# Causal mask, row scale and row extreme of attention scores in one VectorE pass per token tile

## The reference, cut to what matters

```
q = rms_norm((x @ Wq).reshape(B, S, 16, 128), gq)
k = rms_norm((x @ Wk).reshape(B, S, 4, 128), gk)      # then each repeated 4 times
attn = einsum('bqhd,bkhd->bhqk', q, k) * 128 ** -0.5
attn = where(causal, attn, -inf);  attn = softmax(attn, axis=-1)
out = einsum('bhqk,bkhd->bqhd', attn, v).reshape(B, S, 2048) @ Wo
```

## Time and profile before

| | |
|---|---|
| median of 3 runs | 1098.98 us (1098.12 to 1102.88) |
| the profiled execution | 1098.61 us |
| its span, first to last instruction | 1096.7 us |
| PE (matmuls) busy | 1002.0 us, 91% |
| DVE busy | 729.3 us, 66% |
| ACT busy | 691.1 us, 63% |
| mean granted clock of TensorE | 0.961 of full |

### The profile page before, as it was taken

The page is one execution under the profiler, slowest core; times in us unless marked ns, Lnnn a source line. Parts: engine busy times, 40 slices in busy tenths (PEclk is TensorE's granted clock), DMA queues, the critical chain, the costliest instruction groups (busy, mean ns, idle before and its releaser), DMA issues.

```text
span 1096.7 us, 20605 instructions
## 1 busy us (share of the span) xinstructions
PE 1002.0 (91%) x6148; PEld 837.5 (76%) x6148; DVE 729.3 (66%) x2417; ACT 691.1 (63%) x1944; POOL 427.8 (39%) x450
## 2 busy tenths in 40 slices
PE   7999999999999999999999999985788688999990
PEld 4668888877887788887887788864567587999990
DVE  3564656777748766774884686765677666888880
ACT  2567767777767676866776686663544346676760
POOL 3222411425412541541263253231064643666663
PEclk9999999999999999999999999997789799999995
DMA  9919992986894200110021031227066678899964
GB/s 312 284 61 332 378 376 73 354 299 252 301 377 149 109 20 1 65 64 1 1 90 40 1 131 55 84 93 251 11 166 158 172 167 224 220 228 228 232 144 77
DMA packets 93725, 180.47 MB, mean 165 GB/s; under 512 B 9949, under 2 KB 29085, under 8 KB 92717
## 3 DMA queue, kind: packets, MB, share of 16 engines
q1 hardware_dynamic: 73467, 148.55, 40.6%
q0 software_dynamic: 18800, 30.24, 12.0%
q10 hardware_dynamic: 1346, 0.36, 0.2%
HBM read 77.58 MB, written 107.99 MB: 169 GB/s over the span
## 4 chain that ended last, share of the span: by engine, by line
PE 78%; DVE 8%; DMA 4%; issue 3%; ACT 3%; another core or an unknown queue 1%; POOL 1%; SPq 0%; DVEq 0%; ACTq 0%; POOLq 0%
PE bank L1071 11%; PE bank L1007 10%; PE bank L1035 9%; PE bank L1080 6%; PE bank L1025 4%; PE bank L995 4%; PE bank L983 3%; PE bank L860 3%; PE bank L954 2%; PE bank L994 2%; PE bank L869 2%; PE bank L1026 2%; PE bank L1016 2%; DMA X<-xsD 2%; PE bank L938 2%
## 5 line engine op out<-in xcount | busy, mean ns | idle before, releaser
L1867 POOL TENSOR_TENSOR RB<-RB 128x512 f32<-128x512 f32 x64 | 67.6, 1056 | 251.4 <-DVE RB L1649 249.1
L1071 PE MATMUL bank<-RB 128*128 128x128 f32 x1264 | 161.4, 283 | 3.6 <-ACT RB L1347 3.0
L1071 PEld LDWEIGHTS bank<-RB 128*128 128x128 f32 x1264 | 155.8, 200 | 6.4 <-ACT RB L1347 4.4
L1035 PE MATMUL bank<-RA,RB 128*128 128x256 f32 x512 | 132.7, 382 | 1.7 <-ACT RB L1241 1.7
L1340 ACT ACTIVATE RB<-RA,nw 128x512 f32 x158 | 105.5, 715 | 35.2 <-issue 17.6
L1007 PE MATMUL bank<-RA 128*128 128x256 f32 x512 | 123.0, 384 | 0.0
L1007 PEld LDWEIGHTS bank<-RA 128*128 128x128 f32 x512 | 95.6, 192 | 15.5 <-issue 2.4
L1035 PEld LDWEIGHTS bank<-RA,RB 128*128 128x128 f32 x512 | 89.2, 190 | 17.8 <-issue 2.8
L1843 POOL TENSOR_TENSOR qs<-qs,half 128x4 f32<-128x4 f32 x64 | 64.9, 1015 | 90.2 <-DVE qs L1658 71.9
L1080 PE MATMUL bank<-RB,BC 128*128 128x256 f32 x316 | 86.1, 398 | 14.5 <-DVE BC L1774 14.5
L1893 POOL DMA_INDIRECT xsD<-SC,pu x64 | 63.9, 998 | 66.9 <-DVE pu L1585 51.2
(11 more groups left out here) (261 smaller groups left out, 2421.8 us busy)
## 6 DMA issues: line engine op xcount, KB each, us to landing
xsD<-BC SPq DMA_DIRECT2D x17, 4232.0 KB, 32.5
RB<-in_w2b SPq DMA_DIRECT2D x79, 256.0 KB
RB<-xsD SPq DMA_DIRECT2D x55, 264.5 KB, 3.6
BC<-modD SPq DMA_DIRECT2D x16, 512.0 KB, 4.5
X<-xsD SPq DMA_DIRECT2D x24, 264.5 KB, 3.1
RA<-in_w SPq DMA_DIRECT2D x2, 2048.0 KB
RA<-in_w SPq DMA_DIRECT2D x6, 512.0 KB
RA<-in_L_attn_Wq SPq DMA_DIRECT2D x1, 2048.0 KB, 13.3
```

Of the source, the lines that this page charges most:

```text
L1035: m = pe.matmul(bank[5][:, t * 256:t * 256 + 256], OT[:, u % 2, t * 128:t * 128 + 128], Wo[:, h, :], start=(h == 0 and t == 0), stop=(h == ...
L1071: m = pe.matmul(ps[:, 128 * j:128 * j + 128], WS[:, n % 2, c, 128 * j:128 * j + 128], XT[:, n % 2, c * 128:c * 128 + 128], start=(c == 0), ...
L1867: pool.tensor_tensor(sq, qrow, qrow, ALU.mult).then_inc(mine("q_sq", p), 1)
```

## The change

The mask product L997 goes. `s_max` becomes two `tensor_tensor_reduce` instructions: each reads scores in PSUM and a constant mask in SBUF, adds them, multiplies by the row scale, writes the result to P in SBUF, and gives the minimum of each row. The gain product changes its sign, so that scores arrive negated and the mask is +1e30; the minimum is then the bias that the exponential wants. `s_exp` reads P and writes P, without the row scale. The waits move with this: `s_max` waits for the row scale before its first instruction, for the constants, and for the transposes of unit u-4 that free its P; the bank is released by `s_max`; `q_rs` waits for `s_max`. The constant tile has six blocks of 128 columns in place of four. The scheduler's cost of `scores` is .67 in place of .78; those of `s_max` (.84) and `s_exp` (1.15) stay.

```diff
-              "p_t .33 scores .78 q_mm 1.73 ...
+              "p_t .33 scores .67 q_mm 1.73 ...
...
-            yield do("q_rs", n, after=[("s_exp", 2 * n - 3)] * (n >= 2))
+            yield do("q_rs", n, after=[("s_max", 2 * n - 3)] * (n >= 2))
...
-        yield do("s_max", u, bank=1 + u % 2, after=[("q_rs", u // 2)])
-        yield do("s_exp", u, bank=1 + u % 2, last=True, after=[("p_t", u - 4)] * (u >= 4))
+        yield do("s_max", u, bank=1 + u % 2, last=True, after=[("q_rs", u // 2)] + [("p_t", u - 4)] * (u >= 4))
+        yield do("s_exp", u)
...
-        cb16 = sb("cb16", [128, 128 * 4], BF16)
-        identb, triadd, ustrict, ones_b = (cb16[:, 128 * i:128 * i + 128] for i in range(4))
+        cb16 = sb("cb16", [128, 128 * 6], BF16)
+        identb, ustrict, ones_b = (cb16[:, 128 * i:128 * i + 128] for i in range(3))
+        causal = cb16[:, 384:768]
...
             def scores(u):
-                on.wait_ge(L["cb16"], 32)
...
-                pe.matmul(ps[:, 0:128], q[:, 0:128], k[:, 0:128], start=True, stop=False, skip_group_check=True)
-                pe.matmul(ps[:, 128:384], q[:, 128:256], k[:, 0:256], start=False, stop=False, skip_group_check=True)
-                diagonal = ps[:, :].rearrange("p (t n) -> p t n", t=2)[:, :, 0:128]
-                pe.matmul(diagonal, identb, triadd.unsqueeze(1).broadcast_to([128, 2, 128]), start=False, stop=True, skip_group_check=True).then_inc(mine("scores", u), 1)
+                pe.matmul(ps[:, 0:128], q[:, 0:128], k[:, 0:128], start=True, stop=True)
+                pe.matmul(ps[:, 128:384], q[:, 128:256], k[:, 0:256], start=True, stop=True).then_inc(mine("scores", u), 1)
...
             def s_exp(u):
                 on.wait_ge(*done("s_max", u))
-                on.wait_ge(*done("q_rs", u // 2))
-                if u >= 4:
-                    on.wait_ge(*done("p_t", u - 4))
-                act.activation(P[:, u % 4, 0:128], ps[:, 0:128], ACT.Exp, bias=s[:, 2:3], scale=rq[:, 0:1], accum_out=s[:, 4:5])
-                act.activation(P[:, u % 4, 128:384], ps[:, 128:384], ACT.Exp, bias=s[:, 3:4], scale=rq[:, 1:2], accum_out=s[:, 5:6]).then_inc(mine("s_exp", u), 1)
+                act.activation(P[:, u % 4, 0:128], P[:, u % 4, 0:128], ACT.Exp, bias=s[:, 2:3], scale=-1.0, accum_out=s[:, 4:5])
+                act.activation(P[:, u % 4, 128:384], P[:, u % 4, 128:384], ACT.Exp, bias=s[:, 3:4], scale=-1.0, accum_out=s[:, 5:6]).then_inc(mine("s_exp", u), 1)
...
-                    dve.tensor_tensor(gqk[:, 2:3], gqk[:, 0:1], gqk[:, 1:2], ALU.mult).then_inc(ch.sem, ch.up())
+                    dve.scalar_tensor_tensor(gqk[:, 2:3], gqk[:, 0:1], -1.0, gqk[:, 1:2], ALU.mult, ALU.mult).then_inc(ch.sem, ch.up())
...
             def s_max(u):
                 on.wait_ge(*done("scores", u))
-                dve.tensor_reduce(s[:, 0:1], ps[:, 0:128], AXX, ALU.max).then_inc(ch.sem, ch.up())
-                dve.tensor_reduce(s[:, 1:2], ps[:, 128:384], AXX, ALU.max).then_inc(ch.sem, ch.up())
-                on.wait_ge(ch.sem, ch.n)
                 on.wait_ge(*done("q_rs", u // 2))
-                dve.scalar_tensor_tensor(s[:, 2:4], s[:, 0:2], -1.0, rq, ALU.mult, ALU.mult).then_inc(mine("s_max", u), 1)
+                on.wait_ge(L["cb16"], 32)
+                if u >= 4:
+                    on.wait_ge(*done("p_t", u - 4))
+                dve.tensor_tensor_reduce(P[:, u % 4, 0:128], ps[:, 0:128], causal[:, 0:128], rq[:, 0:1], 1e38, ALU.add, ALU.min, s[:, 2:3]).then_inc(ch.sem, ch.up())
+                dve.tensor_tensor_reduce(P[:, u % 4, 128:384], ps[:, 128:384], causal[:, 128:384], rq[:, 1:2], 1e38, ALU.add, ALU.min, s[:, 3:4]).then_inc(mine("s_max", u), 1)
...
             def q_rs(p):
-                    on.wait_ge(*done("s_exp", 2 * p - 3))
+                    on.wait_ge(*done("s_max", 2 * p - 3))
...
-    tri = (k[None, :] > k[:, None]) * np.float32(-1e30)
-    c["cb16"] = np.concatenate([np.eye(128), tri, k[None, :] > k[:, None], np.ones((128, 128))], 1).astype(np.float32)
+    tri = (k[None, :] > k[:, None]) * np.float32(1e30)
+    c["cb16"] = np.concatenate([np.eye(128), k[None, :] > k[:, None], np.ones((128, 128)), tri, 0 * tri, tri], 1).astype(np.float32)
```

More of the change, by code:

```diff
@@ L49 @@
         "PE": "n_mm .25 n_pre .2 n_sel .95 x_t .25 h_mm 1.8 y_mm .95 g_t .25 g_mm .95 h_t .45 k_mm 1.72 v_mm 1.72 k_t .45 mod_mm 1.72 modc_mm 3.6 f_t .45 f_gate .9 f_rank .4 s_mm 1.2 s_t .22 d_mm .3 d_t .42 d_y 2.15 "
-              "p_t .33 scores .78 q_mm 1.73 q_t .45 pv .65 wo .87 qk_mm 1.73 vv_mm .87 ls_mm .65 num .56 o1_t .22 wo1 .87",
+              "p_t .33 scores .67 q_mm 1.73 q_t .45 pv .65 wo .87 qk_mm 1.73 vv_mm .87 ls_mm .65 num .56 o1_t .22 wo1 .87",
         "ACT": "w_in 1.65 x_out .38 e_tanh .43 g_out .4 h_mod 1.05 k_sq 1.6 v_out .6 f_ht .62 f_hb .62 f_sig .2 f_sq .9 f_src .9 f_gb .6 f_exp .7 s_tanh .3 s_at .38 d_tanh .32 d_at .7 "
@@ L1208, in s_exp @@
             def s_exp(u):
-                ps, s = bank[1 + u % 2], sm[:, u % 4, :]
-                rq = qs[:, (u // 2) % 2, 4 + 2 * (u % 2):6 + 2 * (u % 2)]
+                s = sm[:, u % 4, :]
                 on.wait_ge(*done("s_max", u))
-                on.wait_ge(*done("q_rs", u // 2))
-                if u >= 4:
-                    on.wait_ge(*done("p_t", u - 4))
-                act.activation(P[:, u % 4, 0:128], ps[:, 0:128], ACT.Exp, bias=s[:, 2:3], scale=rq[:, 0:1], accum_out=s[:, 4:5])
-                act.activation(P[:, u % 4, 128:384], ps[:, 128:384], ACT.Exp, bias=s[:, 3:4], scale=rq[:, 1:2], accum_out=s[:, 5:6]).then_inc(mine("s_exp", u), 1)
+                act.activation(P[:, u % 4, 0:128], P[:, u % 4, 0:128], ACT.Exp, bias=s[:, 2:3], scale=-1.0, accum_out=s[:, 4:5])
+                act.activation(P[:, u % 4, 128:384], P[:, u % 4, 128:384], ACT.Exp, bias=s[:, 3:4], scale=-1.0, accum_out=s[:, 5:6]).then_inc(mine("s_exp", u), 1)
             def p_tout(u):
```

## The result

| | before | after |
|---|---|---|
| median | 1098.55 us (4 runs) | 1073.10 us (4 runs, 1071.31 to 1075.92) |
| ratio, 95% interval | | 0.9748 [0.9726, 0.9770] |
| profiled span | 1096.7 | 1069.5 |
| last `wo` of the 128 units | 739.4 | 704.0 |

The sign and the mask's part were right. Most of the rest came from the new order of the stages, which I had priced on the losing side only.

The account below looks back on a forecast made before the run. PE, busy 97% of the first stage, was taken to bound the kernel there. From 1098.6, -14.0 (mask product), -1.5 (earlier bank release) and +1.5 (DVE) gave 1084.6, stated as 1084.9 us, 1.3% faster; range 1077 to 1097.

Parts of the forecast that it names:

- the mask's part: The 128 mask products leaving PE in the first stage: 14.0 us less.
- What leaves PE: First stage: each of 128 mask products takes 0.11 us of PE; -14.0 us, bounds 0 and -14.0.
- The bank is released earlier: PE's four waits for exponentials to free a bank, 3.4 us in all, shrink: -1.5 us, between 0 and -3.4.
- DVE: The two passes and their reads take 0.85 us a unit against 0.71, mostly hidden: +1.5 us, bounds 0 and +6.
- ACT: Exponentials reading SBUF with one scalar take 0.12 us less a unit, 15 us less on ACT, worth nothing at PE.
- Waits that move: On DVE, s_max now waits for POOL's row scale before its first pass; the scale should be there already: 0.
- the sum: 1098.6 - 14.0 - 1.5 + 1.5 = 1084.6 us, stated as 1084.9; the second stage keeps its 357 us.
- the planner as a rival: The planner reorders all engines, leaving one or two more DVE holes, 7.7 to 14 us: 1093 to 1099; chance 0.16.
- More than the mask is won: Rival: PE's first-stage idle time shrinks by a third, the seam's hole closes by half: -6 and -4, 1075; chance 0.13.
- What would show it: Signs of right: first stage about 14 us shorter, DVE passes near 350 and 484 ns, second stage 357 +-3.
- the seam longer than 20 us: Sign of wrong: over 20 us at the seam, where before DVE waited 7.7 us between 732.8 and 740.55.
- Half rate: Rival: DVE's new passes run at half rate, s_max takes 1.25 us against 0.71, 69 us more on DVE: 1108; chance 0.08.

## Why the prediction was wrong, point by point

- **"What leaves PE", -14.0.** Right within the noise: 13.3 measured in the old order, with 9.4 to 17.2 as its interval.
- **"The bank is released earlier", -1.5.** Right in mechanism and sign. In the old order the four waits of 3.1 to 3.5 us went entirely, not by 1 us each at most, but waits for VectorE grew in their place, so PE's idle time fell by 1.3 us. The times say about -3, and it is no better known than that.
- **"DVE", +0.14 us a unit and +1.5.** The passes were right: 346 and 479 ns against 351 and 484. The reads were not. The rule of the Trainium skill, page "VectorE: DVE Perf Modes", section "Two Vector instructions with no wait between them", that there are two instructions, agrees with the trace (83 ns each). I drew from it the higher half of my bounds, and the read costs nothing, since the next pass starts with it. The unit takes 0.67, which was the value "if that is free". With the stalls of L1668 gone as well, DVE's busy time fell by 13.2 us where I had 18 more. The term should have been slightly negative. The charge itself, 0.08 us for each of DVE's, is not contradicted: 0.15 was measured, with an error as large.
- **"ACT", 0.12 us less a unit.** Right: 398 and 499 ns; ACT's busy time fell by 16.
- **"Waits that move", 0.** The first pass waited for POOL's row scale twice, 1.7 us in all; no more.
- **The failing step** is in the sum: "This moves forward as a whole with the end of the units, if the planner keeps batch element 5 where it is", and "the second stage then keeps its 357 us". The planner did not keep it. It made a new list of 4324 stages, brought the last `wo` 35 us forward, not 14, and left 19 more of PE's stages for after it. The sum had no term for this. The second stage grew from 357 to 365.5 us. The net of it, 12 to 13 us, is shown by the same instructions in either order. I had the planner as a rival, but only as one that takes away, "1093 to 1099"; that rests on one hole in an order that was itself a poor draw. A rival that can go both ways needed both ends: the orders drawn here for the changed instructions lie from 18 us above the old order to 25 us below it (1.0020 and 0.9629 against 0.9854).
- **"More than the mask is won", 1075, 0.13.** Its time came out, 2 us beyond, but in part by luck: its mechanism holds for the first stage (PE's idle time halved, where it said a third less) and not for the hole at the seam, which did not close: 11.9 us of idle there became 11.2. The first 24 blocks gave what the seam did not (4.4 us less idle).
- **"What would show it."** Of the signs of being right, the passes, the exponentials and the missing product came; the first stage was shorter by 35 us and not by 14, and the second took 365.5 us and not 357 +-3. One sign of being wrong came too, "the seam longer than 20 us": it was 40.5, in a faster kernel, because PE is busy for 29.3 of them. The length of the seam says nothing without the work in it.
- **Half rate.** It did not occur; the page of the Trainium skill that I cited for it ("Vector Engine (DVE) Microarchitecture Reference", "Points that are easy to get wrong") speaks of two SBUF sources that are not bf16, and PSUM with bf16 ran at full rate.

Added up in ratios: 0.0121 for the product, about 0.003 for the release and the shorter instructions (inside the noise), about 0.011 for the order (0.9854 in the old one, 0.974 in the new), which is 13, 3 and 12 us.

What stays open: which of the moved stages make the 12 us. No run moved one stage alone. The traces show only where PE idles less: before the last `wo`, and in the first 24 blocks.

## What to carry to other kernels

Where a planner writes the order of all engines, a small edit is two changes: its own, and a new draw of the order. Lay out both orders before the forecast and compare where the stages fall. Price both changes, with a range on either side for the second (here from +2% to -2% beside the edit's own effect), and test them apart by running the new instructions in the old order. And where an engine is busy 97% of a stage, the distance between starts, not the length of a record, is the price of an instruction on it.

## What the runs showed of the hardware that I had not expected

The pass that adds, scales, writes and reduces takes 349 ns for 128 columns and 480 for 256 (medians), the time of a plain two-stream pass of that size with a scalar; its accumulator read (83 ns) lies wholly beside the next pass. A `scalar_tensor_tensor` on two columns with both inputs in SBUF (L1668), 161 ns at the median, took up to 1684. In the kernel before, 9 of its 128 took over 400 ns, and each of the 9 ended within 0.03 us of the end of a POOL `tensor_tensor`. The longest and its POOL instruction:

```profile
256.91 1.68 DVE L1668 SCALAR_TENSOR_TENSOR sm<-sm,qs 128x2 f32<-128x2 f32 x1
257.45 1.11 POOL L1880 TENSOR_TENSOR SC<-SC,BC 128x512 f32<-128x512 f32 x1
```

No new pass, with one input in PSUM, was above 353 or 484 ns in the changed kernel.
